# Attention with a quantised feed-forward on one core: the order of ScalarE's small copies among its exponentials

## The chip, the cores and the metric

The kernel runs on one core of one Trainium2 chip. Its engines are TensorE (matrix products, PE in the rows; PEld is its weight load), VectorE (DVE), ScalarE (ACT), GpSimd (POOL) and SyncE (SP), which issues most transfers. Each runs its own instructions in order, and they wait for each other on semaphores. The metric is the device time of the program in microseconds, the median of several executions; less is better.

## What is computed

For x of shape (8, 512, 1024) and a mask of shape (8, 1024), attention runs over the 1024 positions with 16 heads of 32 channels, and its result goes through an int8 feed-forward layer and is added to x. Cut to what matters:

```python
Q, K, V = (proj(Wq), proj(Wk), proj(Wv))              # each (8, 16, 1024, 32)
att = einsum('bhqd,bhkd->bhqk', Q, K) / sqrt(32) + b
att = softmax(att * m + (1.0 - m) * -1e30, axis=-1)   # m: the mask over keys
y = einsum('bhqk,bhkd->bhqd', att, V)                 # back to (8, 512, 1024)
scale = maximum(max(abs(y), axis=-1), 1e-7) / 127     # of each channel's row
q = clip(round(y / scale), -128, 127)
out = x + float16((q @ weight.T) * scale * w_scale + bias)
```

## The kernel before

The first part (`project`, some 590 us) makes queries, keys and values for the eight batches and stores queries and keys in DRAM, each as a high and a low part. The second part (`attend`) is what the change touches. It runs 32 steps of 53.8 us; a step is four heads of one batch. A step has 64 units, `t` from 0 to 63. A unit is one head, one tile of 128 keys and 512 of the 1024 queries: units 0 to 31 take the first query half, 32 to 63 the second, and four units in a row share a key tile.

For each unit TensorE makes a score tile of 128 by 512 (L798), which carries the mask's bias and the row's maximum in extra rows, so that ScalarE only has to take its exponential into `probs` (L932). Score tiles lie in three PSUM banks in turn: the score of unit t needs the bank that the exponential of unit t - 3 has emptied. (From unit 27 on the banks are counted one further, so unit 28 follows unit 27's.) With each unit TensorE also makes one row-maximum product (L147) into a ring of four PSUM banks, which VectorE reduces (L154). These maxima run ahead: from unit 20 (`OWN`) on they are those of the next step, heads 0 to 3 of the first query half at units 20, 28, 36 and 44, and then the second half.

The units come in bursts of eight. Behind every fourth unit of eight (3, 11, 19, 27, 35, ...) TensorE makes the weighted sums of the values for two key tiles (`weigh`, L829, 16 matmuls, 1.9 us) into the one bank `pv`. Extras stand at fixed units: the maxima are transposed at units 20 and 52 (L169), ScalarE (L176) and VectorE (L182) split them; sums of the probabilities go out at 27 and 59 (L839); the feed-forward of the step before stands at unit 59 (L872).

ScalarE walks the same units. Among its exponentials stand, at numbered units:

- `take_y` (L937), which empties `pv` into `y_raw` once a query half's weighted sums are done: at unit 3 for the step before, at unit 35 for this step's first half. It waits for TensorE's last `weigh` of that half. TensorE's next `weigh` into `pv`, at unit 43, waits for it.
- `double_k` (L963), which copies the 32 rows of the high key part of one head to other partitions, once a head, for the next step: two of them at unit 19 (heads 0 and 1), two at unit 27 (heads 2 and 3). TensorE waits for head h's copy (`k_doubled`) at the first maximum of that head, units 20, 28, 36, 44. They wait for `k_loaded`.
- `double_q2` (L973), the same for two heads of the second query half: at unit 35, behind `take_y`, and at unit 59. It waits for `q2_loaded`. TensorE's maxima of the second query half wait for it (`q2_doubled`), from unit 52 on.
- `round_rows` (L944) at unit 43 and `make_ints` (L949) at 51, which quantise.

SyncE issues the two loads of the second query half of the next step (L117) behind the store of this step's maxima (L189), which is ready a little after unit 20. GpSimd sums the probabilities (L1177), starts adding transfers among them (L1161), normalises and adds bias and residual; it waits for TensorE's weighted sums behind unit 59 once a step. The copies for a step are made in the step before; steps 1 to 30 have them at these units.

Of the kernel before, what the change touches and what calls it, by code (L numbers as in the profile page):

```python
# [28 lines left out]
GH = P // DH  # L29
# [53 lines left out]
def wait(eng, sem, value):  # L83

    if not isinstance(value, int) or value > 0:
        eng.wait_ge(sem, value)


def score_bank(s, t):

    if isinstance(s, int) and s == LAST and t > SKEW:
        return (t - SKEW - 1 + SCORES) % (SCORES + 1)
    return (t - (t > SKEW)) % SCORES
# [39 lines left out]
def landed(all_parts, n):  # L133

    return all_parts + (all_parts - 16) * (n - 1)
# [36 lines left out]
def high_max(nc, act, buf, max_parts, marks, s, chunk, maxT_done, max_rows, max_hi_done):  # L172

    act.wait_ge(maxT_done, 2 * s + chunk + 1)
    wait(act, max_rows[chunk], MAX_ROWS * s)
    nc.scalar.activation(max_parts[:, chunk, :], buf[0:2 * CHUNK, 0:P], ACT.Identity, scale=marks[:, 1:2]).then_inc(max_hi_done, 1)  # L176
# [412 lines left out]
def attend(nc, x, qk_d, v_d, bias_d, fw, ws_rep, fb_rep, out,  # L589
# [5 lines left out]
    with ExitStack() as ctx:  # L595
# [62 lines left out]
        def halves_before(s, half):  # L658

            return QH * s + half  # L660

        def pairs_before(s, half, i):

            return s * sum(i in paired for paired in PAIRED) + half * (i in PAIRED[0])

        def ring_of(use):

            return ring[PLACE[use] % RINGS]
# [14 lines left out]
        def uses(s, par):  # L683

            return (s - par) // 2 + 1
# [233 lines left out]
        @block.scalar  # L919
        def _(act):  # L920
            def exps(s, t):
                half, kt, h = t // (TT * GH), t // GH % TT, t % GH
                if h == 0:

                    wait(act, pv_done, QH * TT * s + t // GH - RING + 1)
                    before = halves_before(s, half) - 1
                    if kt in FREED[1 - half]:
                        wait(act, acc_done, ADDS * before + FREED[1 - half][kt])
                    else:
                        wait(act, pair_done[kt // 2], 16 * pairs_before(s, half, kt // 2))  # L930
                act.wait_ge(score_done, UNITS * s + t + 1)
                nc.scalar.activation(probs[:, kt, h, :], score[score_bank(s, t)][:, :], ACT.Exp).then_inc(exp_done, 1)  # L932

            def take_y(s, half):
                act.wait_ge(pv_done, QH * TT * s + (half + 1) * TT)
                wait(act, y_done, 2 * (s - 1) + half + 1)
                nc.scalar.activation(y_raw[:, half, :], pv[:, :], ACT.Copy).then_inc(y_raw_done, 1)  # L937

            def round_rows(s, cols=slice(0, T)):

                if s == 0:
                    act.wait_ge(const_set, 3)
                act.wait_ge(inv_done, s + 1)
                nc.scalar.activation(y[:, cols], y[:, cols], ACT.Identity, bias=magic[:, 0:1], scale=inv_scale[:, 0:1]).then_inc(rounded, 1)  # L944

            def make_ints(s, cols=slice(0, T)):
                act.wait_ge(rounded, s + 1)
                wait(act, qT_done, s)
                nc.scalar.activation(q_int[:, cols], y[:, cols], ACT.Identity, bias=magic[:, 1:2]).then_inc(q_done, 1)  # L949

            def store_out(s, half):
                act.wait_ge(res_done, 2 * s + half + 1)
                act.dma_start(out[s * P:(s + 1) * P, half * N:(half + 1) * N],
                              res[:, half * N:(half + 1) * N]).then_inc(out_stored, 16)

            def load_res(s):

                wait(act, out_stored, 32 * s)
                act.dma_start(res[:, :], x[s * P:(s + 1) * P, :]).then_inc(res_loaded, 16)

            def double_k(s, h):
                act.wait_ge(k_loaded[s % 2], landed(LOADS_K, uses(s, s % 2)))
                nc.scalar.activation(k_stack[s % 2][2 * DH:3 * DH, h, :], k_stack[s % 2][0:DH, h, :].bitcast(F32),  # L963
                                     ACT.Copy).then_inc(k_doubled, 1)

            def double_q1(s):
                act.wait_ge(q1_loaded[s % 2], landed(LOADS_Q, uses(s, s % 2)))
                nc.scalar.activation(q_stack[s % 2][DH:2 * DH, 0, :, :], q_stack[s % 2][0:DH, 0, :, :].bitcast(F32),
                                     ACT.Copy).then_inc(q1_doubled, 1)

            def double_q2(s, i):
                act.wait_ge(q2_loaded[s % 2], landed(LOADS_Q, uses(s, s % 2)))
                nc.scalar.activation(q_stack[s % 2][DH:2 * DH, 1, 2 * i:2 * i + 2, :],  # L973
                                     q_stack[s % 2][0:DH, 1, 2 * i:2 * i + 2, :].bitcast(F32), ACT.Copy).then_inc(q2_doubled, 1)

            def step(s, prev=True, ahead=True):
                for t in range(UNITS):
                    exps(s, t)
                    if prev and ahead and t == 19:
                        double_k(s + 1, 0)  # L980
                        double_k(s + 1, 1)
                    if prev and ahead and t == 27:
                        double_k(s + 1, 2)
                        double_k(s + 1, 3)
                    if t == GH - 1 and prev:
                        take_y(s - 1, 1)
                    if t == TURN_1:
                        high_max(nc, act, ring_of(("turn", t)), max_parts, marks, s, 1, maxT_done, max_rows, max_hi_done)
                    if t == UNITS // 2 + GH - 1:
                        take_y(s, 0)  # L990
                    if prev and ahead and t == 35:
                        double_q2(s + 1, 0)
                    if prev and ahead and t == SUMS_0:
                        double_q2(s + 1, 1)
                    if s + 2 < STEPS and t == SUMS_0:
                        double_q1(s + 2)
                    if t == ROUND and prev:
                        round_rows(s - 1)
                    if t == INTS and prev:
                        make_ints(s - 1)  # L1000
                        if s >= 2:
                            store_out(s - 2, 1)
                    if t == SUMS_0 and prev:
                        load_res(s - 1)
                    if t == TURN_0 and ahead:
                        high_max(nc, act, ring_of(("turn", t)), max_parts, marks, s + 1, 0, maxT_done, max_rows, max_hi_done)

            for i in range(2):
                act.wait_ge(part_stored[i], 16 * B * STAGES)
            for s in range(STEPS):  # L1010
                step(s, prev=s > 0, ahead=s < LAST)
            round_rows(LAST, slice(0, N))
            make_ints(LAST, slice(0, N))
# [289 lines left out]
```

## Time and profile before

| | us |
|---|---|
| median of 3 runs | 2297.32 (2295.03 to 2297.74) |
| the profiled execution | 2295.35 |
| its span | 2293.5 |

Busy in the span: TensorE 98%, GpSimd 74%, VectorE 70%, ScalarE 67%. TensorE's share comes from matmuls whose ends are modelled, and the shares are means over two parts with different limits, so a step of the second part is read by itself: the order of each engine's instructions in time, with its idle time and who ended it. The step from 1354.00 to 1407.83 us is read below; the period is 53.81 to 53.92 us in all the steps from 1 to 30. It begins with the feed-forward at unit 59; unit 4 is at 1362.95, unit 12 at 1368.74, unit 20 at 1374.54, unit 28 at 1381.63, unit 36 at 1387.44 and unit 44 at 1394.41.

### The profile page before, as it was taken

What the parts mean: (1) busy time and instruction counts of PE and PEld (TensorE: products, weight loads), DVE (VectorE), ACT (ScalarE), POOL (GpSimd) and SP (SyncE); (2) the same over time, 40 slices, a digit from 0 to 9 for tenths busy, and PEclk for the clock granted to TensorE, in tenths of its full rate; (3) what the DMA queues carried; (4) which work ended last, traced back from release to release, by engine and by line L of the source; (5) the groups of instructions that cost most, each with busy time, mean ns of one, the idle gap of its engine ahead of it and who ended that gap; (6) DMA issues with size and microseconds to landing.
All of it is one profiled execution on the core that took longest, in us unless ns stands there. A gap on an engine that the chain in (4) does not pass through costs nothing.

```text
span 2293.5 us, 34614 instructions
## 1 busy us (share of the span) xinstructions
PE 2249.3 (98%) x11892; PEld 1354.8 (59%) x11924; DVE 1616.1 (70%) x2779; ACT 1538.4 (67%) x2681; POOL 1708.3 (74%) x735
## 2 busy tenths in 40 slices
PE   9999999999999999999999999999999999999998
PEld 7888888887555555555555555555555555555553
DVE  3311111117888888888888888888888888888883
ACT  3322222223788888887887888888888887888774
POOL 2322333322899998989999998998989989998996
PEclk9999999999999999999999999999999999999999
DMA  6665545575888888888888888888888888888874
GB/s 238 253 229 193 183 183 215 189 219 145 188 186 188 185 185 189 185 191 189 194 187 189 178 189 183 190 187 187 187 184 187 189 188 191 189 189 189 181 155 109
DMA packets 137909, 433.27 MB, mean 189 GB/s; under 512 B 12248, under 2 KB 48088, under 8 KB 113440
## 3 DMA queue, kind: packets, MB, share of 16 engines
q0 software_dynamic: 27360, 199.24, 44.2%
q1 hardware_dynamic: 101040, 205.85, 29.5%
q10 hardware_dynamic: 9360, 26.22, 3.2%
q8 instruction: 91, 1.49, 0.3%
q14 instruction: 58, 0.48, 0.1%
HBM read 130.06 MB, written 100.93 MB: 101 GB/s over the span
## 4 chain that ended last, share of the span: by engine, by line
PE 91%; ACT 3%; POOL 2%; DMA 2%; issue 1%; DVE 0%; POOLq 0%; ACTq 0%
PE score L798 21%; PE pv L829 20%; PE ring L147 19%; PE ring L344 11%; PE score L344 9%; PE ring L872 4%; PE pv L344 3%; PE ring L839 2%; POOL acc L1177 2%; DMA probs<-probs 1%; ACT q_stack L973 1%; ACT probs L932 1%; PE ring L862 1%; ACT y_raw L937 1%; PE ring L169 0%
## 5 line engine op out<-in xcount | busy, mean ns | idle before, releaser
L154 DVE TENSOR_REDUCE half_max<-ring 128x1 f32<-128x512 f32 x2048 | 1261.9, 678 | 92.2 <-PE ring L147 84.4
L932 ACT ACTIVATE probs<-score 128x512 f32<-128x512 f32 x2039 | 1032.6, 615 | 235.0 <-PE score L798 233.5
L1177 POOL TENSOR_TENSOR acc<-acc,probs 128x2048 f32<-128x2048 f32 x189 | 903.6, 4781 | 29.0 <-DMA probs<-probs 26.9
L798 PE MATMUL score<-q_stack,k_stack 100*128 100x512 f32 x2039 | 855.6, 421 | 25.0 <-ACT probs L932 25.0
L147 PE MATMUL ring<-k_stack,q_stack 98*128 98x512 f32 x2048 | 815.1, 398 | 1.7 <-issue 1.7
L798 PEld LDWEIGHTS score<-q_stack,k_stack 100*128 100x128 f32 x2039 | 383.2, 188 | 386.3 <-issue 184.4
L829 PE MATMUL pv<-probs,v_in 128*32 128x512 f32 x4096 | 492.5, 598 | 0.0
L147 PEld LDWEIGHTS ring<-k_stack,q_stack 98*128 98x128 f32 x2048 | 388.4, 190 | 65.0 <-DVE qT L1084 9.0
L1177 POOL TENSOR_TENSOR acc<-probs 128x2048 f32<-128x2048 f32 x63 | 297.8, 4727 | 30.3 <-DMA probs<-probs 15.6
L562 POOL TENSOR_TENSOR q_stack<-x_raw,k_stack 128x1024 fp32r<-128x1024 f32 x28 | 67.8, 2462 | 294.0 <-ACT k_stack L426 294.0
L1161 POOL DMA_DIRECT2D probs<-probs x190 | 192.4, 1012 | 102.8 <-PE pv L829 92.2
L829 PEld LDWEIGHTS pv<-probs,v_in 128*32 128x32 f32 x4096 | 106.9, 109 | 231.8 <-ACT probs L932 143.9
L502 DVE TENSOR_TENSOR part_lo<-score,part_hi 128x512 fp32r<-128x512 f32 x24 | 16.2, 690 | 181.1 <-ACT part_hi L453 181.1
L576 POOL TENSOR_TENSOR part_lo<-k_scaled,part_hi 128x512 fp32r<-128x512 f32 x64 | 82.3, 1304 | 55.3 <-ACT part_hi L456 55.3
L963 ACT ACTIVATE k_stack<-k_stack 32x1024 fp32r<-32x1024 f32 x120 | 120.1, 1047 | 1.5
L456 ACT ACTIVATE part_hi<-k_scaled 128x512 fp32r<-128x512 f32 x64 | 39.3, 629 | 115.9 <-DVE k_scaled L513 87.4
L872 PE MATMUL ring<-fw,qT 128*128 128x512 bf16 x480 | 108.8, 379 | 5.9 <-issue 4.9
L344 PE MATMUL ring<-q_stack,w_hi 128*128 128x512 f32 x256 | 101.3, 396 | 0.0
L344 PE MATMUL ring<-k_stack,w_lo 128*128 128x512 f32 x256 | 101.2, 395 | 0.0
L1184 POOL TENSOR_TENSOR y<-y_raw,factor 128x512 f32<-128x512 f32 x63 | 98.4, 1562 | 2.2 <-DVE factor L1037 2.2
L344 PE MATMUL ring<-k_stack,w_hi 128*128 128x512 f32 x256 | 99.5, 396 | 0.0
L1190 POOL TENSOR_TENSOR half<-prod,fb_rep 128x512 f16<-128x512 f32 x63 | 89.2, 1416 | 12.9 <-DVE prod L1089 12.9
(118 smaller groups left out, 2117.6 us busy)
## 6 DMA issues: line engine op xcount, KB each, us to landing
probs<-probs POOLq DMA_DIRECT2D x190, 1024.0 KB, 8.4
q_stack<-qk_part SPq DMA_DIRECT2D x132, 256.0 KB, 4.3
k_stack<-qk_part SPq DMA_DIRECT2D x66, 512.0 KB
qk_part<-part_hi SPq DMA_DIRECT2D x64, 512.0 KB, 2.7
qk_part<-part_lo SPq DMA_DIRECT2D x64, 512.0 KB, 3.6
v_steps<-v_out SPq DMA_DIRECT2D x64, 256.0 KB, 2.3
v_in<-v_steps SPq DMA_DIRECT2D x32, 512.0 KB, 4.7
v_out<-x ACTq DMA_DIRECT2D x31, 512.0 KB, 8.1
```

The costliest lines, as they stand in the source:

```text
L147: pe.matmul(bank[:, :], q_stack[par][0:ROW_MAX, chunk, h, qt * P:(qt + 1) * P], k_stack[par][0:ROW_MAX, h, half * N:(half + 1) * N], start ...
L154: nc.vector.tensor_reduce(half_max[:, pair // CHUNK, pair % CHUNK, half:half + 1], bank[:, :], AX_X, ALU.max, negate=True).then_inc(neg_ma ...
L344: return pe.matmul(bank[:, :], lhsT, rhs, start=(k == 0), stop=(k == 3 * CT - 1))
L798: pe.matmul(score[score_bank(s, t)][:, :], k_stack[par][0:ROWS, h, kt * P:(kt + 1) * P], q_stack[par][0:ROWS, half, h, :], start=True, sto ...
L829: mm = pe.matmul(pv[h * DH:(h + 1) * DH, :], v_in[:, par, kt % TT, h * DH:(h + 1) * DH], probs[:, kt % RING, h, :], start=(kt % TT == 0), ...
L872: mm = pe.matmul(buf[:, :], qT[:, tt, :], fw[:, tt, cols], start=(tt == 0), stop=(tt == TT - 1))
L932: nc.scalar.activation(probs[:, kt, h, :], score[score_bank(s, t)][:, :], ACT.Exp).then_inc(exp_done, 1)
L963: nc.scalar.activation(k_stack[s % 2][2 * DH:3 * DH, h, :], k_stack[s % 2][0:DH, h, :].bitcast(F32), ACT.Copy).then_inc(k_doubled, 1)
L1161: pool.dma_start(probs[:, b, :, :], probs[:, a, :, :], accum_op=ALU.add).then_inc(pair_done[i], 16)
L1177: nc.gpsimd.tensor_tensor(acc[:, half, :, :], first, probs[:, tile, :, :], ALU.add).then_inc(acc_done, 1)
L1184: nc.gpsimd.tensor_tensor(y[:, half * N:(half + 1) * N], y_raw[:, half, :], factor[:, half, :], ALU.mult).then_inc(y_done, 1)
L1190: nc.gpsimd.tensor_tensor(half16[:, half, :], prod[:, half, :], fb_rep[:, half * N:(half + 1) * N], ALU.add).then_inc(half_done, 1)
```

## The change

In ScalarE's step, three edits. `double_k` of head 1 moves from unit 19 to unit 27, where it stands ahead of those of heads 2 and 3. The `double_q2` of unit 35 is written ahead of `take_y` instead of behind it. All other work, its waits and its data stay as they are.

```diff
                     if prev and ahead and t == 19:
                         double_k(s + 1, 0)
-                        double_k(s + 1, 1)
                     if prev and ahead and t == 27:
-                        double_k(s + 1, 2)
-                        double_k(s + 1, 3)
+                        for h in range(1, GH):
+                            double_k(s + 1, h)
+                    if prev and ahead and t == 35:
+                        double_q2(s + 1, 0)
                     if t == GH - 1 and prev:
                         take_y(s - 1, 1)
...
                     if t == UNITS // 2 + GH - 1:
                         take_y(s, 0)
-                    if prev and ahead and t == 35:
-                        double_q2(s + 1, 0)
                     if prev and ahead and t == SUMS_0:
                         double_q2(s + 1, 1)
```

ScalarE's instructions around units 19 to 27, before. The first row is the exponentials of units 4 to 19, L963 the key copies, L176 the split of the maxima behind unit 20, and the seven exponentials are units 21 to 27:

```order
L932 ACTIVATE probs<-score 128x512 x16
L963 ACTIVATE k_stack<-k_stack 32x1024 x2
L932 ACTIVATE probs<-score 128x512
L176 ACTIVATE max_parts<-ring,marks 32x128
L932 ACTIVATE probs<-score 128x512 x7
L963 ACTIVATE k_stack<-k_stack 32x1024 x2
```

The same place after the change:

```order
L932 ACTIVATE probs<-score 128x512 x16
L963 ACTIVATE k_stack<-k_stack 32x1024
L932 ACTIVATE probs<-score 128x512
L176 ACTIVATE max_parts<-ring,marks 32x128
L932 ACTIVATE probs<-score 128x512 x7
L963 ACTIVATE k_stack<-k_stack 32x1024 x3
```

One key copy has gone from ahead of unit 20's exponential to ahead of unit 28's.

ScalarE's instructions around unit 35, before. The first row is the exponentials of units 28 to 35, L937 is `take_y`, L973 the query copy, and the next eight exponentials are units 36 to 43:

```order
L932 ACTIVATE probs<-score 128x512 x8
L937 ACTIVATE y_raw<-pv 128x512
L973 ACTIVATE q_stack<-q_stack 32x1024
L932 ACTIVATE probs<-score 128x512 x8
L944 ACTIVATE y<-y,magic,inv_scale 128x1024
```

After the change:

```order
L932 ACTIVATE probs<-score 128x512 x8
L973 ACTIVATE q_stack<-q_stack 32x1024
L937 ACTIVATE y_raw<-pv 128x512
L932 ACTIVATE probs<-score 128x512 x8
L944 ACTIVATE y<-y,magic,inv_scale 128x1024
```

The query copy and `take_y` have changed places. The order on TensorE, VectorE and GpSimd is the same in both kernels.

## Rows read from the trace of the kernel before

**Rows 1.** The page: busy time of each engine, and TensorE's granted clock in 40 slices.
```profile
PE 2249.3 (98%) x11892; PEld 1354.8 (59%) x11924; DVE 1616.1 (70%) x2779; ACT 1538.4 (67%) x2681; POOL 1708.3 (74%) x735
...
PEclk9999999999999999999999999999999999999999
```

**Rows 2.** Waits of TensorE over the span: us in total, times, longest us.
```profile
PE score L798 <- ACT probs L932: 25.0, 32, 0.8
```

**Rows 3.** Busy time by stretches: length, busy us (instructions) by engine, clock, DMA, GB/s.
```profile
1354.00:1407.83 53.83, 52.86 (x298) 28.48 (x298) 46.84 (x83) 43.82 (x78) 48.92 (x21) 1.00 0.87 187
```

**Rows 4.** TensorE in order of time, units 36 to 44: start, us, instruction [idle before].
```profile
1387.44 0.50 PE L798 MATMUL score<-q_stack,k_stack 100*128 100x512 f32 x1
...
1388.73 0.39 PE L147 MATMUL ring<-k_stack,q_stack 98*128 98x512 f32 x1
1389.93 0.50 PE L798 MATMUL score<-q_stack,k_stack 100*128 100x512 f32 x1 [0.81 <-ACT probs L932]
1390.27 0.40 PE L147 MATMUL ring<-k_stack,q_stack 98*128 98x512 f32 x1
...
1394.41 0.50 PE L798 MATMUL score<-q_stack,k_stack 100*128 100x512 f32 x1
```

**Rows 5.** ScalarE in order of time, behind unit 19 to unit 43, repeats merged.
```profile
1373.41 2.00 ACT L963 ACTIVATE k_stack<-k_stack 32x1024 fp32r<-32x1024 f32 x2
1375.43 0.60 ACT L932 ACTIVATE probs<-score 128x512 f32<-128x512 f32 x1
...
1376.18 3.44 ACT L932 ACTIVATE probs<-score 128x512 f32<-128x512 f32 x7
1379.64 2.00 ACT L963 ACTIVATE k_stack<-k_stack 32x1024 fp32r<-32x1024 f32 x2
1382.25 4.03 ACT L932 ACTIVATE probs<-score 128x512 f32<-128x512 f32 x8 [0.61 <-PE score L798]
1387.58 0.60 ACT L937 ACTIVATE y_raw<-pv 128x512 f32<-128x512 f32 x1 [1.30 <-PE pv L829]
1388.20 1.06 ACT L973 ACTIVATE q_stack<-q_stack 32x1024 fp32r<-32x1024 f32 x1
1389.28 4.03 ACT L932 ACTIVATE probs<-score 128x512 f32<-128x512 f32 x8
```

**Rows 6.** TensorE in order of time: units 12, 20, 23, 24, 28 and 31.
```profile
1368.74 0.50 PE L798 MATMUL score<-q_stack,k_stack 100*128 100x512 f32 x1
...
1374.54 0.50 PE L798 MATMUL score<-q_stack,k_stack 100*128 100x512 f32 x1
...
1376.43 0.40 PE L147 MATMUL ring<-k_stack,q_stack 98*128 98x512 f32 x1
1376.81 0.50 PE L798 MATMUL score<-q_stack,k_stack 100*128 100x512 f32 x1
...
1381.63 0.50 PE L798 MATMUL score<-q_stack,k_stack 100*128 100x512 f32 x1
...
1383.14 0.40 PE L798 MATMUL score<-q_stack,k_stack 100*128 100x512 f32 x1
```

**Rows 7.** ScalarE in order of time, behind unit 3 and at unit 4.
```profile
1363.08 0.60 ACT L937 ACTIVATE y_raw<-pv 128x512 f32<-128x512 f32 x1 [1.30 <-PE pv L829]
1363.58 0.59 ACT L932 ACTIVATE probs<-score 128x512 f32<-128x512 f32 x1
```

**Rows 8.** Query loads of L117: their slowest step at this place, then the line's whole span.
```profile
L117 SPq DMA_DIRECT2D q_stack<-qk_part x2: 329/352/375, 1539.1 to 1539.6; - x2
...
DMA to landing us min/median/max: 3.9/4.7/5.5
...
DMA to landing us min/median/max: 3.0/4.3/12.1
```

**Rows 9.** VectorE in order of time: the reductions of units 44 to 51.
```profile
1395.18 4.88 DVE L154 TENSOR_REDUCE half_max<-ring 128x1 f32<-128x512 f32 x8 [0.36 <-PE ring L147]
```

**Rows 10.** GpSimd in order of time: its shortest wait behind unit 59, in steps 1 to 30.
```profile
1622.79 0.85 POOL L1161 DMA_DIRECT2D probs<-probs  x1 [1.47 <-PE pv L829]
```

## The prediction

> **What bounds the kernel now.** I read the page first. TensorE is busy for 98% of the span at a granted clock of full speed, the 2.4 GHz level, in all forty slices [rows 1]; the clock is not what this change can move. Of one step of the attention part (units 0 to 63) the table by stretches shows 53.83 us, of which TensorE is busy for 52.86, GpSimd for 48.92, VectorE for 46.84, ScalarE for 43.82, and the DMA engines for 0.87 of the time [rows 3]. So TensorE sets the period, and what can be won is the time in which it stands still. Next I read who it waits for: over the whole span 25.0 us in 32 times, for ScalarE's exponentials, 0.8 us at the longest [rows 2]. The order of TensorE's work in one step then tells where: between the row maximum of unit 38 (1388.73) and the score of unit 39 (1389.93) it stands still for 0.81 us [rows 4]. The trace has this row, of 0.81 to 0.83 us, in each of the 30 steps 1 to 30; they make 24.5 of the 25.0 us.
>
> The reason is a chain of three PSUM banks. The score of unit 39 goes into the bank that the exponential of unit 36 empties. ScalarE is idle for 1.30 us behind the exponential of unit 35, until TensorE has finished the weighted sums that `take_y` copies (1387.58); then it copies, then it does the query copy of 1.06 us (1388.20), and only then the exponential of unit 36 (1389.28) [rows 5]. The query copy, which depends on none of this, stands on the path, and the hole of 1.30 us in front of it is empty.
>
> **What a stall costs beside its idle time.** Behind an undisturbed burst of eight units the next burst's first score comes 5.80 us after this one's (1368.74 to 1374.54) [rows 6]. For the burst of unit 36 it is 6.97 us (1387.44 to 1394.41) [rows 4]. The burst therefore costs 1.17 us too much and not 0.81: the first maximum behind the stall comes 0.34 us after its score (1389.93, 1390.27) [rows 4] where six matmuls take 1.51 us without a stall (1381.63 to 1383.14, its first one 0.34 as well, so 0.235 each behind it) [rows 6], the matmul in front of the stall ends earlier than its slot, and the four scores behind it follow ScalarE's pace of 0.48 us.
>
> **Part 1, the query copy in front of `take_y`.** After the change it follows the exponential of unit 35: the eight exponentials from 1382.25 last 4.03, so they end at 1386.28 [rows 5]. It is a move; nothing is added. It then holds ScalarE from 1386.3 for 1.08 (from 1388.20 to 1389.28 in rows 5) to 1387.4, and `take_y` cannot begin before 1387.58 anyway. Its cover is the 1.30 us hole, with 0.2 us left. The exponential of unit 36 comes 0.50 us behind the start of `take_y`, as at unit 4, where no copy stands between (1363.08, 1363.58) [rows 7]: at 1388.08. The release takes 0.65 us from the start of an exponential to the matmul that needs its bank (1389.28 to 1389.93) [rows 4, 5], and some 0.1 more until the stream is back in its slots, so unit 39 could go at 1388.83; undisturbed it is due 1.51 us behind 1387.44, at 1388.95 [rows 4, 6]. The stall is gone, with 0.12 us to spare: gain 1.17 us a step. The lower bound of this gain is the idle row alone, 0.81.
>
> The copy waits for the loads of the next step's second query half (`q2_loaded`). That wait now has `take_y` and the exponentials queued behind it, and TensorE behind those. In the slowest step that I found, the second of the two loads was issued at 1539.6 and landed 5.5 us later [rows 8]; three steps of 53.84 earlier this is 1383.6, and the copy is due at 1386.3, so 2.7 us are left. No cost.
>
> **Part 2, one key copy from unit 19 to unit 27.** Now two copies stand behind unit 19 (1373.41) and the exponential of unit 20 starts at 1375.43; its score was started at 1374.54 and would let it start 0.62 later (unit 28 does: 1381.63, 1382.25) at 1375.16 [rows 5, 6]. It is 0.27 late, the turned maxima follow, and unit 21's exponential is at 1376.18. TensorE pays at unit 24: 0.38 us between 1376.43 and 1376.81 in place of 0.235, and the 0.10 of a restart: 0.25 us [rows 5, 6]. With one copy this goes, as everything from unit 20 on moves 0.27 earlier on ScalarE: gain 0.25.
>
> Behind unit 27 three copies stand in place of two. The two start at 1379.64 and take 2.00, and the one before unit 20's exponential shows 2.02 from the first copy to it [rows 5]; three take about 2.99. They start 0.27 earlier, at 1379.37, so unit 28's exponential starts at 1382.36, while its score, 0.25 earlier, has it ready at 1382.00. It is 0.36 late. Unit 31's score needs its bank at 1383.14 less 0.25, 1382.89, and can go at 1382.36 plus 0.74, 1383.10 [rows 5, 6]: 0.21 lost, and four more units at ScalarE's 0.48 in place of 0.47 and a late weight load at the end lose some 0.07. The second part thus gives 0.25 and takes 0.28: net minus 0.03. The bounds are plus 0.25 (nothing lost at unit 31) and minus 0.25 (the gain at unit 24 absent). The key copies' own reader is no cost: TensorE takes head 1 behind unit 28's score (1381.63) and that copy now ends near 1380.4; heads 2 and 3 are taken at units 36 and 44.
>
> **The sum.** 1.17 less 0.03 is 1.14 us in each of 30 steps, 34.2 us. The profiled execution took 2295.35, so 2261.1; the median lies 2.0 above it, and the forecast is 2263.1.
>
> **What is late next.** GpSimd keeps its place from step to step by one wait, for TensorE's weighted sums behind unit 59; its idle time there was 1.47 us in the tightest of the steps [rows 10], and about 3.5 in most. 1.14 fits in. VectorE is closer: behind unit 43 it waits 0.36 us for TensorE [rows 9], and that wait will be about zero, since it has all of its work of unit 39 (maximum of the outputs, scales) still to do while TensorE comes 1.17 earlier. Then only the four ring banks, nearly two units of room, stand between a late reduction and TensorE.
>
> A rule of the Trainium skill speaks here ("Perfetto Trace Analysis", section "Identifying the Most-Contended Engine"): TensorE's busy share is no good measure, since pipelined matmuls are misread, while for GpSimd occupancy is a fair one; the most occupied engine is to be improved first. By that rule GpSimd (48.92 of 53.83) would be the bound and a better order on ScalarE would bring little. This trace speaks against it, since GpSimd waits for TensorE in every step; it is rival 3 below.
>
> **Rivals.**
> 1. VectorE or a rest of the stall takes part of the gain in the second half of the step, so that only about the idle row comes back: 0.81 times 30 is 24.3, time 2273. For it: VectorE's vanished slack [rows 9]. Against: four banks. Chance 0.16.
> 2. Unit 31 loses nothing: 1.17 plus 0.25 is 1.42, times 30 is 42.6, time 2254.7. For it: unit 20's exponential, 0.27 late in the trace, goes by without idle time of TensorE in front of unit 23, which waits for it; the bubble comes at unit 24. Against: 0.36 is more than 0.27. Chance 0.12.
> 3. GpSimd becomes the bound, because its transfers land later when they are asked for in less time: the gain shrinks to under 0.5 us a step, 2282 to 2297. Chance 0.05, since it needs its 1.47 to 4 us of slack gone.
> 4. Slower: a late load holds the query copy, and with it `take_y`. The longest landing on that line is 12.1 us [rows 8]; issued at 1378.1 (1539.6 less three steps) it is there at 1390.2, `take_y` starts at 1391.3 and unit 36's exponential at 1391.8 in place of 1389.28: 2.5 us a step, 75 us, time 2372 if it is so in all steps. It decides from a landing of 9.6 us after the issue on. The 12.1 is of other loads on the same line; those at this place took up to 5.5. Chance 0.03.
> 5. The move has no effect, because the 1.30 us hole isn't idle on ScalarE but hides a release that the copy only shifts: time 2297. Against: unit 3 shows the same hole and no stall. Chance 0.02.
>
> **How the numbers follow.** Forecast, 2259 to 2268: 0.62. From 0.2% on (4.6 us, about what a measurement of this kernel tells from no change) it counts as faster: forecast and rivals 1 and 2, and most of 3, 0.94; within 0.2%: 0.03; slower 0.03. Leaving out rivals 3 to 5 leaves 0.9, so the range runs from 2254 (rival 2) to 2273 (rival 1).
>
> **What would show it.** Right: TensorE's waits for the exponentials fall from 25.0 us to below 5; the query copy starts right behind unit 35's exponential, `take_y` at its old place behind unit 35's weighted sums; period 52.7; a small bubble at unit 31 and none at unit 24. Wrong: idle time in front of the query copy (rival 4), TensorE's weight loads waiting for VectorE's reductions (rival 1), GpSimd's wait behind unit 59 at zero (rival 3).

## The result

| | us |
|---|---|
| before, median of 7 runs | 2296.71 (2295.03 to 2301.94) |
| changed, median of 7 runs | 2303.70 (2295.93 to 2304.62) |
| ratio changed to before | 1.002, 95% interval 1.001 to 1.0029 |
| the changed kernel's profiled execution | 2295.93 (its span 2294.1) |

The change made the kernel slower by 0.2% (0.3% between the two medians), where I had forecast 1.5% faster. The profiled execution is the fastest of the seven, 8 us under the median; the other six lie between 2302.9 and 2304.6. So the trace below shows the mechanism, but less of the loss than the median holds: its execution is only 0.6 us longer than the one profiled before.

The page of the changed kernel has VectorE, ScalarE and GpSimd about as busy as before, and TensorE 12.7 us busier [rows 1]:

```profile
span 2294.1 us, 34646 instructions
PE 2262.0 (99%) x11924; PEld 1359.3 (59%) x11924; DVE 1612.4 (70%) x2779; ACT 1541.7 (67%) x2681; POOL 1709.8 (75%) x735
```

TensorE has no more work than before. Its 32 more instructions are records of the feed-forward that are missing in the trace before (7.3 us), and the row maxima (L147) show 13.7 us more for the same 2048 matmuls, which is where the new waits are.

The waits over the span (us in total, times, longest) show that the stall which the change aimed at is gone, 25.0 us in [rows 2] and 0.4 now, and what has come in its place:

```profile
POOL acc L1176 <- DMA probs<-probs: 110.3, 73, 10.5
...
DVE absmax L1041 <- POOL y L1183: 45.4, 36, 10.2
...
ACT y L944 <- DVE inv_scale L1054: 27.7, 15, 7.5
...
PE ring L147 <- DVE half_max L154: 14.8, 19, 1.8
...
PE ring L798 <- ACT probs L932: 4.0, 2, 3.8
...
PE score L798 <- ACT probs L932: 0.4, 2, 0.2
```

Before, the first three were these:

```profile
POOL acc L1177 <- DMA probs<-probs: 42.5, 60, 2.8
...
DVE absmax L1042 <- POOL y L1184: 8.9, 2, 7.5
ACT y L944 <- DVE inv_scale L1055: 8.4, 2, 7.6
```

GpSimd waits 68 us more for its adding transfers, VectorE 37 us more for GpSimd's normalised outputs (L1183, `normalise`), ScalarE 19 us more for the scales that VectorE makes of them (L1054), and TensorE waits for VectorE's reductions.

**The steps fall into two kinds.** From one feed-forward's start to the next, the 29 steps before took 53.81 to 53.92 us. Now eleven of the first 29 take 52.62 to 52.74 us, as forecast, while thirteen take 53.5 to 56.8, with stalls of TensorE around unit 24 or 44 or both; the mean is 53.77, against 53.85 before. First a step that went as it should have, ScalarE in order of time from behind unit 27 on, the rows that answer to [rows 5]:

```profile
1055.31 2.95 ACT L963 ACTIVATE k_stack<-k_stack 32x1024 fp32r<-32x1024 f32 x3
1058.28 4.03 ACT L932 ACTIVATE probs<-score 128x512 f32<-128x512 f32 x8
1062.33 1.05 ACT L973 ACTIVATE q_stack<-q_stack 32x1024 fp32r<-32x1024 f32 x1
1063.54 0.60 ACT L937 ACTIVATE y_raw<-pv 128x512 f32<-128x512 f32 x1 [0.16 <-PE pv L829]
1064.04 4.02 ACT L932 ACTIVATE probs<-score 128x512 f32<-128x512 f32 x8
```

The query copy fills the hole in front of `take_y`, 0.16 us of it is left (forecast 0.2), and unit 36's exponential follows `take_y` by 0.50. TensorE's scores of units 20, 28, 31, 36 and 44 in the same step answer to [rows 4, 6]:

```profile
1050.48 0.50 PE L798 MATMUL score<-q_stack,k_stack 100*128 100x512 f32 x1
...
1057.30 0.50 PE L798 MATMUL score<-q_stack,k_stack 100*128 100x512 f32 x1
...
1058.93 0.50 PE L798 MATMUL score<-q_stack,k_stack 100*128 100x512 f32 x1
...
1063.41 0.50 PE L798 MATMUL score<-q_stack,k_stack 100*128 100x512 f32 x1
...
1069.20 0.50 PE L798 MATMUL score<-q_stack,k_stack 100*128 100x512 f32 x1
```

Units 36 to 44 take 5.79 us instead of 6.97: 1.18 won, forecast 1.17. Units 20 to 28 take 6.82 instead of 7.09: 0.27 won, forecast 0.25. Units 28 to 36 take 6.11 instead of 5.81: 0.30 lost, forecast 0.28, though not where I had put it: unit 31's score comes 0.12 late (1.63 behind unit 28's in place of 1.51; forecast 0.21), and the other 0.18 is lost behind it. Each of the three parts came out to within 0.02 us, and the means over all eleven such steps are the same to 0.01.

**The loop that binds now.** GpSimd in order of time in the same step, from one issue of pair 1's transfer for the second half to the next. (Pair i is the adding transfer of key tile 2i onto 2i + 1, L1160 here. Pair 1 of the second half is the last but one issued in a step, ahead of GpSimd's wait behind unit 59; GpSimd's second sum of the half needs it.)

```profile
1025.98 1.26 POOL L1160 DMA_DIRECT2D probs<-probs  x1
1029.59 0.86 POOL L1160 DMA_DIRECT2D probs<-probs  x1 [2.34 <-PE pv L829]
...
1036.18 4.58 POOL L1176 TENSOR_TENSOR acc<-acc,probs 128x2048 f32<-128x2048 f32 x1 [1.17 <-DMA probs<-probs]
...
1054.96 4.58 POOL L1176 TENSOR_TENSOR acc<-probs 128x2048 f32<-128x2048 f32 x1 [0.40 <-DMA probs<-probs]
...
1076.05 4.59 POOL L1176 TENSOR_TENSOR acc<-acc,probs 128x2048 f32<-128x2048 f32 x1 [1.17 <-DMA probs<-probs]
1080.59 0.86 POOL L1160 DMA_DIRECT2D probs<-probs  x1
```

GpSimd waits 2.34 us for TensorE behind unit 59 (1029.59), which reads as slack. But it is no slack: the transfer of pair 1 has been issued in front of that wait (1025.98), and its landing, 10 us later, holds the second sum (1036.18) whatever TensorE does. Had TensorE come 1 us earlier and the landing stayed where it was, the 2.34 would be 1.34 and the 1.17 would be 2.17. From there on everything on GpSimd follows in one chain: sum, bias and residual, sum, pair 0 and its landing (0.40), sums, normalising, pair 3 and its landing (1.17), the last sum, and pair 1 again. One turn took 54.61 us (1025.98 to 1080.59), while TensorE's step took 52.63. Such a turn puts GpSimd 2 us behind TensorE. The next turn takes 51.69 us; over the 29 steps the turns lie between 50.5 and 58.0, and their mean is that of the steps, 53.8.

A slow step shows how this reaches TensorE. VectorE takes the maximum of each output half at fixed places in its order, at units 19 and 39, and there waits for GpSimd's `normalise`. The step from 973.1 on, GpSimd first, then VectorE, then TensorE:

```profile
980.72 4.59 POOL L1176 TENSOR_TENSOR acc<-acc,probs 128x2048 f32<-128x2048 f32 x1 [2.42 <-DMA probs<-probs]
...
1001.90 4.60 POOL L1176 TENSOR_TENSOR acc<-probs 128x2048 f32<-128x2048 f32 x1 [2.87 <-DMA probs<-probs]
...
1011.60 1.57 POOL L1183 TENSOR_TENSOR y<-y_raw,factor 128x512 f32<-128x512 f32 x1
```

```profile
994.50 0.69 DVE L1041 TENSOR_REDUCE absmax<-y 128x1 f32<-128x512 f32 x1 [0.59 <-POOL y L1183]
...
1013.21 0.69 DVE L1041 TENSOR_REDUCE absmax<-y 128x1 f32<-128x512 f32 x1 [2.88 <-POOL y L1183]
```

```profile
1015.07 0.47 PE L147 MATMUL ring<-k_stack,q_stack 98*128 98x512 f32 x1 [1.70 <-DVE half_max L154]
```

Two landings cost GpSimd 2.42 and 2.87 us, its output comes at 1013.2, VectorE stands still for 2.88 us with the ring's maxima behind it, the four ring banks fill, and TensorE stands still for 1.70 us at unit 44.

There is a second way, and it shows in the step behind the 29, the 30th. The scales wait for the same maximum, ScalarE's rounding (L944, unit 43) waits for the scales, and the exponentials stand behind the rounding. ScalarE, then TensorE:

```profile
2252.33 1.24 ACT L944 ACTIVATE y<-y,magic,inv_scale 128x1024 f32<-128x1024 f32 x1 [3.58 <-DVE inv_scale L1054]
```

```profile
2254.10 0.80 PE L798 MATMUL ring<-q_stack,k_stack 100*128 100x512 f32 x1 [3.79 <-ACT probs L932]
```

Before, the two waits at this place were 0.88 and 1.07 us. This step took 56.1 us, before 51.9. So in the profiled execution the 29 steps together are 2.3 us shorter than before, and the 30th alone is 4.2 us longer.

**The clock falls behind such a stall.** TensorE's table by stretches (length, busy us by engine, granted clock, DMA, GB/s) around it:

```profile
1012.90:1016.30 3.40, 1.70 (x10) 0.88 (x7) 3.03 (x7) 1.93 (x3) 3.40 (x5) 1.00 0.19 39
1016.40:1019.80 3.40, 3.40 (x9) 2.56 (x9) 3.40 (x7) 2.46 (x5) 3.40 (x2) 0.50 1.14 231
```

In the first stretch TensorE is busy for 1.70 of 3.40 us; in the second it runs at the 1.2 GHz level and makes 9 matmuls. At the 2.4 GHz level it makes 14 in that time (0.235 us each), so such a fall costs up to 1.7 us more, on top of the stall (an estimate: half of the 3.4). The granted clock shows 0.50 in the same way at 1716 and 1986 us, behind stalls of 1.56 and 1.75 us, and for 6.8 us from 2252.0 on, inside the stall of 3.79; behind a stall of 1.26 us it did not fall. In the attention part of the kernel before it fell in the last 1.3 us alone. The length of a stall does not settle it: in the traces of the experiments below, stalls of 1.78 us (`after_add_cut`, at 1015.6) and 2.25 us (`after_absmax_late`, at 1722.4) had no fall behind them, and one of 1.19 us (`after_pair2_later`, at 1448.3) had. The mean granted clock of the seven runs is 0.993 to 0.998.

### The profile page after: what moved, and what is told of

It reads as the page before. It is cut to its first block, busy times and chain, and to the rows that moved or that the text cites. A ratio compares the mean times of both kernels' runs of the same rounds, so it can differ in the third digit from the quotient of the medians.

```text
span 2294.1 us, 34646 instructions
## 1 busy us (share of the span) xinstructions
PE 2262.0 (99%) x11924; PEld 1359.3 (59%) x11924; DVE 1612.4 (70%) x2779; ACT 1541.7 (67%) x2681; POOL 1709.8 (75%) x735
## 4 chain that ended last, share of the span: by engine, by line
PE 83%; issue 7%; POOL 4%; DMA 3%; ACT 2%; DVE 1%; POOLq 0%; ACTq 0%
PE score L798 18%; PE ring L147 17%; PE pv L829 16%; PE ring L344 11%; PE score L344 9%; PE ring L872 4%; DMA probs<-probs 3%; PE pv L344 3%; PE ring L839 2%; POOL acc L1176 2%; ACT probs L932 1%; POOL y L1183 1%; PE ring L862 1%; DVE absmax L1041 1%; DVE half_max L154 0%
## 5 line engine op out<-in xcount | busy, mean ns | idle before, releaser
L147 PE MATMUL ring<-k_stack,q_stack 98*128 98x512 f32 x2048 | 828.8, 405 | 16.6 <-DVE half_max L154 14.8
L147 PEld LDWEIGHTS ring<-k_stack,q_stack 98*128 98x128 f32 x2048 | 390.3, 191 | 112.1 <-DVE half_max L154 45.1
L1160 POOL DMA_DIRECT2D probs<-probs x190 | 194.8, 1026 | 44.7 <-PE pv L829 37.3
L963 ACT ACTIVATE k_stack<-k_stack 32x1024 fp32r<-32x1024 f32 x120 | 120.2, 1047 | 1.5
L872 PE MATMUL ring<-fw,qT 128*128 128x512 bf16 x512 | 116.1, 380 | 0.8 <-DVE qT L1083 0.8
L1183 POOL TENSOR_TENSOR y<-y_raw,factor 128x512 f32<-128x512 f32 x63 | 98.5, 1563 | 2.1 <-DVE factor L1036 2.1
```

What stands on the lines that cost most here:

```text
L147: pe.matmul(bank[:, :], q_stack[par][0:ROW_MAX, chunk, h, qt * P:(qt + 1) * P], k_stack[par][0:ROW_MAX, h, half * N:(half + 1) * N], start ...
L872: mm = pe.matmul(buf[:, :], qT[:, tt, :], fw[:, tt, cols], start=(tt == 0), stop=(tt == TT - 1))
L1160: pool.dma_start(probs[:, b, :, :], probs[:, a, :, :], accum_op=ALU.add).then_inc(pair_done[i], 16)
L1183: nc.gpsimd.tensor_tensor(y[:, half * N:(half + 1) * N], y_raw[:, half, :], factor[:, half, :], ALU.mult).then_inc(y_done, 1)
```

## The experiments

Theory A, formed from the rows above: GpSimd and its adding transfers form a loop that takes 53 to 55 us a step, the 53.85 of TensorE before hid it, and it binds once TensorE wants 52.7. The rivals: the key copies' move costs (B), the clock falls for another reason and is the cause (C), GpSimd's total work is the bound (D), and some more that stand with their runs. Controls apply the same edit to the kernel before.

### The two parts apart

`q_only` takes the query copy alone (the edit is against the changed kernel):

```diff
                     if prev and ahead and t == 19:
                         double_k(s + 1, 0)
+                        double_k(s + 1, 1)
                     if prev and ahead and t == 27:
-                        for h in range(1, GH):
-                            double_k(s + 1, h)
+                        double_k(s + 1, 2)
+                        double_k(s + 1, 3)
```

> Only the query copy in front of take_y at unit 35; the key copies as before. Theory A (a GpSimd and transfer loop of 53.5 to 54 us a step has become the bound: pair 1's transfer of the second half, issued in front of GpSimd's wait behind unit 59, lands too late for the second sum): the stall at unit 39 goes, steps of 52.7 us alternate with late ones, and the time is within 0.4% of before, 2290 to 2305. Rival B (moving three key copies behind unit 27 is what costs; the query copy alone brings 1.1 us a step): 2262 to 2266.

Measured: 2299.60 us, ratio 1.0014 (1.0004 to 1.0023). Rival B falls: the query copy alone, forecast to gain 35 us, loses 3 to 4. `k_only` takes the other part alone, from the kernel before:

```diff
                     if prev and ahead and t == 19:
                         double_k(s + 1, 0)
-                        double_k(s + 1, 1)
                     if prev and ahead and t == 27:
-                        double_k(s + 1, 2)
-                        double_k(s + 1, 3)
+                        for h in range(1, GH):
+                            double_k(s + 1, h)
```

> Only head 1's key copy from unit 19 to unit 27; the query copy stays behind take_y. Theory A: TensorE's period stays at 53.8 us or so, GpSimd keeps its slack, 2294 to 2299. Rival B (the key copies cost): 2335, since it would have to eat the 34 us of the query copy and 7 more.

Measured: 2295.88 us, ratio 0.9999 (0.9989 to 1.0008), clock 0.999, the stall at unit 39 in every step as before. Where unit 39's stall sets the step, the key copies are worth nothing either way.

### Taking work out of the loop, and beside it

`after_bias_cut` shortens GpSimd's bias addition, which lies in the loop. It leaves out the bias on 448 of each 512 columns in all steps but the last (one memset at the start fills them):

```diff
...
-                nc.gpsimd.tensor_tensor(half16[:, half, :], prod[:, half, :], fb_rep[:, half * N:(half + 1) * N],
+                few = 64 if s is not LAST else N
+                nc.gpsimd.tensor_tensor(half16[:, half, 0:few], prod[:, half, 0:few], fb_rep[:, half * N:half * N + few],
                                         ALU.add).then_inc(half_done, 1)
```

> The changed kernel, with GpSimd's bias addition cut to 64 of 512 columns in all steps but the last (work left out: the bias on 448 columns of each half). It takes about 1.2 us twice a step out of GpSimd's chain between the landing of pair 1 and its next issue. Theory A: the loop falls under TensorE's 52.7 us: 2262 to 2268, no long stalls at units 24 and 40, clock 0.999. Rival C (TensorE's clock, which falls in some stretches of the changed kernel for another reason, costs the time): as the changed kernel, 2300 or more.

Measured: 2260.78 us, ratio 0.9849 (0.9833 to 0.9866). All 29 steps of its trace take 52.63 to 52.81 us, and the clock's mean is 0.999. In the trace a shortened addition takes 0.96 us less on the mean, twice a step. The whole forecast gain is there as soon as these 1.9 us of GpSimd's chain are gone, so nothing on TensorE, ScalarE or VectorE hindered it. Rival C falls: with the same order on TensorE and ScalarE the granted clock stays at 1.00 through all the steps read (it falls only in the last 4 us of the span), and the gain is there. Not every fall needs the change: `k_only` and `before_bias_cut`, with the old order of the query copy, have one of 3.4 us in the last step too (at 2242 and 2237).

`before_bias_cut`, the control, is the same edit in the kernel before.

> Control: the kernel before, with the same bias addition cut to 64 of 512 columns in all steps but the last. Theory A: before, TensorE's own 53.85 us a step bind and GpSimd has room, so nothing is won: 2293 to 2297. Rival E (GpSimd's chain was the bound already before, and the cut brings the same at any order of ScalarE's copies): 2262.

Measured: 2294.75 us, ratio 0.9994 (0.9984 to 1.0003). Before, GpSimd did not bind.

`after_add_cut` takes about as much work out, but where GpSimd waits for pair 1's landing anyway. It leaves out two of the four heads in the first addition of each second half, 2.2 us:

```diff
...
-                nc.gpsimd.tensor_tensor(acc[:, half, :, :], first, probs[:, tile, :, :], ALU.add).then_inc(acc_done, 1)
+                heads = slice(0, 2) if (half, k) == (1, 0) else slice(0, GH)
+                first = probs[:, FIRST, heads, :] if k == 0 else acc[:, half, heads, :]
+                nc.gpsimd.tensor_tensor(acc[:, half, heads, :], first, probs[:, tile, heads, :], ALU.add).then_inc(acc_done, 1)
```

> The changed kernel, with the first addition of each second half cut to two of its four heads (work left out: tile 6 and tile 1 of heads 2 and 3 in the row sums of second halves). It takes about 2.4 us out of GpSimd's work, but at the place where GpSimd waits for pair 1's landing anyway. Theory A: the wait grows by what the addition loses, and the time stays near the changed kernel's, 2295 to 2304. Rival D (GpSimd's busy time as a whole is the bound, wherever it is spent): as the bias cut, 2262 to 2268.

Measured: 2295.19 us, ratio 0.9997 (0.9985 to 1.001). GpSimd in order of time, the second sum in the step that answers to the slow one above:

```profile
981.15 4.58 POOL L1179 TENSOR_TENSOR acc<-acc,probs 128x2048 f32<-128x2048 f32 x1 [4.83 <-DMA probs<-probs]
```

The wait has grown from 2.42 to 4.83 us, by at least what the addition lost. Over the span GpSimd's waits for its transfers grew from 110.3 to 162.7 us, by most of the 67 us by which its additions are shorter. Rival D falls: 2.2 us a step less work brought 8.5 us of the median here against the changed kernel, and 1.9 us less brought 43 us at the other place. The Trainium skill ("Perfetto Trace Analysis", section "Identifying the Most-Contended Engine") would have the engine with the highest occupancy improved first, and calls occupancy a fair measure for GpSimd. It would have pointed to the right engine, which I had dismissed. But these two runs show that occupancy does not say what to take off it: GpSimd is busy for 49.0 of 52.6 us in a good step and was for 48.9 of 53.8 before, when it did not bind [rows 3], and what binds is its work and the transfers' landings in one chain.

### Moving things in the loop, with all work kept

`after_fill` puts work into the wait for pair 1's landing:

```diff
-                if prev:
-                    add(s - 1, 1, 1)
                 if second:
                     add_bias(s - 2, 0)
                     add_residual(s - 2, 0)
                 if prev:
+                    add(s - 1, 1, 1)
                     add(s - 1, 1, 2)
```

> The changed kernel, complete, with GpSimd's bias and residual additions of the first half (2.6 us) in front of the second sum of the second half, where it stood idle for pair 1's landing, instead of behind it. Theory A: pair 1 may land 2.6 us later without holding GpSimd, the loop is shorter by 2.6 us than TensorE's period needs, and TensorE's 52.7 us a step bind: 2260 to 2266, clock 0.999, no waits over 0.5 us at units 24 and 40. Rival D (GpSimd's total work is what binds): no change against the changed kernel, 2300 to 2305, since it does exactly the same work.

Measured: 2264.66 us, ratio 0.9868 (0.9851 to 0.9884), with the whole computation. GpSimd in its trace, one step:

```profile
1017.59 1.31 POOL L1160 DMA_DIRECT2D probs<-probs  x1
1021.58 0.86 POOL L1160 DMA_DIRECT2D probs<-probs  x1 [2.69 <-PE pv L829]
1022.14 4.87 POOL L1176 TENSOR_TENSOR acc<-probs 128x2048 f32<-128x2048 f32 x1
1026.65 1.61 POOL L1189 TENSOR_TENSOR half<-prod,fb_rep 128x512 f16<-128x512 f32 x1
1028.42 1.16 POOL L1197 TENSOR_TENSOR v_out<-v_out,half 128x512 f32<-128x512 f32 x1 [0.16 <-POOL half L1189]
1029.54 4.61 POOL L1176 TENSOR_TENSOR acc<-acc,probs 128x2048 f32<-128x2048 f32 x1
```

Pair 1's transfer again takes 10.0 us (its landing in the trace), but the second sum starts 11.95 us behind the issue without a wait, as bias and residual lie between. The 29 steps take 52.67 to 52.80. `q_only_fill` has the same fill, and only the query copy moved.

> The same fill, with only the query copy moved and the key copies as before. It measures what the key copies' move is worth where TensorE binds. From my sum (0.25 won at unit 24, 0.28 lost at unit 31) within 2 us of the run with both, 2260 to 2267; if unit 31 loses nothing, 7 us slower than it.

Measured: 2263.64 us, ratio 0.9862 (0.9845 to 0.9878). Most of its steps take 52.67 to 52.70 against 52.70 to 52.73 with the key copies moved: the key copies' move costs 0.03 us a step, as the sum had it, which is less than the whole times can tell apart. Three of its steps take 53.1 to 55.0, with a stall of 1.21 us for VectorE's reductions in one of them: the fill leaves the loop some room, but not much. `before_fill` is the control.

> Control: the same fill in the kernel before. TensorE binds there with 53.85 us a step and GpSimd's wait behind unit 59 has room: 2293 to 2297.

Measured: 2296.00 us, ratio 0.9999 (0.999 to 1.0009). Neither edit brings anything alone; together they bring 1.3 to 1.4%.

`after_pair_early` issues pair 1 earlier instead:

```diff
                 begin_pair(s, 1, 0)
-                add(s, 0, 3)
                 if ahead:
                     begin_pair(s, 1, 1)
+                add(s, 0, 3)
+                if ahead:
                     begin_pair(s, 1, 2)
```

> The changed kernel, complete, with GpSimd issuing pair 1's transfer of the second half ahead of its last addition of the first half instead of behind it. No work is taken out. GpSimd then waits some 2 us for TensorE's weighted sums behind unit 51, of the 3 it had left behind unit 59, and the transfer starts 4 us earlier and no longer beside pair 2's. Theory A: the late landing is out of the loop, and the time is 2262 to 2272. Rival F (GpSimd's work alone, not the landing, is what the loop consists of): 2295 to 2305, since its work is the same and it waits once more.

Measured: 2282.43 us, ratio 0.9934 (0.9912 to 0.9955): faster than both kernels, but 10 us above the expectation and 18 us short of `after_fill`. GpSimd's waits for its transfers have fallen from 110.3 to 30.3 us over the span, and a new wait has come, TensorE's for the stored maxima of the next step (SyncE's small transfer at L189), at unit 0, 9.8 us in 15 times:

```profile
1460.03 0.50 PE L798 MATMUL score<-q_stack,k_stack 100*128 100x512 f32 x1 [0.55 <-DMA q_stack<-max_parts]
```

That transfer was issued at 1448.41, and pairs 0 and 1 were now both under way (issued at 1444.43 and 1447.24). `before_pair_early` is the control.

> Control: the kernel before with the same earlier transfer of pair 1. Theory A: TensorE's own stall at unit 39 still sets the period of 53.85: 2293 to 2297. Rival H (the earlier transfer shortens any order): 2285 or less.

Measured: 2301.92 us, ratio 1.0027 (1.0017 to 1.0038), slower than both expectations: I had not counted the small transfer. Five of its first 29 steps are 0.6 to 1.3 us longer than 53.85, with a gap at the same place beside that of unit 39.

`after_pair2_later` asks what makes pair 1's landing long, by issuing pair 2 behind the first sum instead of in front of it:

```diff
                 if prev:
+                    begin_pair(s - 1, 1, 2)
                     add(s - 1, 1, 1)
...
                     begin_pair(s, 1, 1)
-                    begin_pair(s, 1, 2)
                     add(s, 1, 0)
```

> The changed kernel, complete, with pair 2's transfer of the second half issued behind GpSimd's first addition of that half (5 us later) instead of in front of it, so that pair 1's, issued 1.6 us before it, travels without it at first. It asks whether pair 1's long landing (9.9 us on the mean, against 8.3 for pair 0's) is due to its company. If it is: pair 1 lands in some 8.3 us, the loop is 1.5 us shorter, time 2265 to 2280. If it isn't: landing stays at 9.5 or more and the time at 2295 to 2304. Pair 2's own landing is needed 9 us after its issue, which may turn into a wait at the third sum.

Measured: 2299.78 us, ratio 1.0014 (1.0002 to 1.0026). Pair 1's mean landing is 9.4 us instead of 9.7, with pair 2 issued 7 us behind it. So it is as long when pair 2 isn't beside it for most of its way, and pair 2 is refuted as what makes it long; what does stays open.

### Taking away the way to TensorE

`after_absmax_late` lets VectorE take the first output half's maximum later, at unit 31 instead of 19:

```diff
-                    if t == TURN_1 - 1 and prev:
-                        take_absmax(s - 1, 0)
-                        take_floor(s - 1)
...
                     if t == SUMS_1 + 4 and prev:
                         spread(s - 1, 1)
+                        take_absmax(s - 1, 0)
+                        take_floor(s - 1)
```

> The changed kernel, with VectorE's maximum of the first output half moved from unit 19 to unit 31. It takes away the way in which a late GpSimd reaches TensorE at unit 24 (VectorE waits for the normalised outputs, the ring of maxima fills). Theory A: GpSimd's loop is as long as before, so TensorE is held elsewhere (unit 40, sums behind 27 and 59); a small gain, 2285 to 2300. Rival G (the wait at unit 20 alone is the cost): 2262 to 2268.

Measured: 2308.00 us, ratio 1.0042 (1.0022 to 1.0063), worse than expected. The stalls at unit 24 are gone from its trace, and those around unit 44 are longer and more: in eight of 29 steps two matmuls there stand 1.7 to 2.8 us apart, in the changed kernel in four. Rival G falls, and it fits a loop: what TensorE doesn't wait for at one place it waits for at the next. That it costs 4 us more than the changed kernel I had not foreseen; the longer stalls bring falls of the clock with them (mean 0.994), but how much is theirs these runs don't part.

## Why the prediction was wrong

- **What bounds the kernel before, the cost of the stall (1.17 us and not 0.81), the query copy's cover, the 0.50 and 0.65 us links, the loads' margin:** right. The good steps show 1.18 us, and no step shows the query copy waiting for its loads (rival 4). The hole in front of `take_y` was idle and took the copy (rival 5).
- **The key copies, net minus 0.03 us a step:** right, 0.27 won and 0.30 lost in the trace, 0.03 between `after_fill` and `q_only_fill`. That the 0.21 at unit 31 was 0.12 and the 0.07 behind it 0.18 cancels out; so far the match is luck. Rival 2 fell.
- **The sum, 34.2 us:** right as TensorE's share. With GpSimd's loop relieved the kernel takes 2260.8 to 2264.7 us, forecast 2263.1.
- **"What is late next" is the step that failed.** It read GpSimd's wait behind unit 59, 1.47 us at the least and some 3.5 in most steps [rows 10], as room for 1.14. The wait stands beside a transfer in flight that doesn't depend on it. The room was what lies between pair 1's landing and the second sum. Before, over the 29 steps, the landing came 4.6 us after the feed-forward's start on the mean, and the second sum at 5.1 where nothing held it: 0.5 us. The trace before says so in GpSimd's rows. At the start of the step that I had read, pair 1 is issued at 1348.99, lands 9.2 us later, at 1358.2, and is needed at 1359.11. In another step (the last two rows) it lands 10.3 us after its issue and holds the second sum for 1.69 us; in eleven of the 29 steps it held it for 0.3 us or more. I had used the issue alone. By this estimate, taking 1.14 us a step from a loop with 0.5 us of room could have given at most 0.5. The rows:

```profile
1348.99 0.85 POOL L1161 DMA_DIRECT2D probs<-probs  x1
1353.59 0.86 POOL L1161 DMA_DIRECT2D probs<-probs  x1 [3.75 <-PE pv L829]
...
1359.11 4.60 POOL L1177 TENSOR_TENSOR acc<-acc,probs 128x2048 f32<-128x2048 f32 x1
...
1727.16 1.13 POOL L1161 DMA_DIRECT2D probs<-probs  x1
...
1737.60 4.60 POOL L1177 TENSOR_TENSOR acc<-acc,probs 128x2048 f32<-128x2048 f32 x1 [1.69 <-DMA probs<-probs]
```

- **Rival 3, given 0.05, is what happened, and its end was too low.** I had it end at no change (2297). A loop that runs late does not merely give the gain back. The mean time to landing of pair 1 went from 9.3 to 9.7 us and that of pair 2 from 11.5 to 13.5, TensorE's waits come in lumps of up to 1.8 us in the 29 steps and of 3.8 in the 30th, and behind some of them the clock falls. The reason given against it, that GpSimd waits for TensorE in every step, is the same misreading.
- **Rival 1 (VectorE takes part of the gain):** wrong as priced. With GpSimd relieved (`after_bias_cut`, `after_fill`) TensorE has no stall for VectorE's reductions in the attention part. It is VectorE, though, through which GpSimd's lateness reaches TensorE. The margin of its first maximum I had not worked out: in the step read before, `normalise` ended at 1372.94 and the maximum began at 1374.57, 1.6 us later.

**Open:** what makes the other executions 8 us longer than the profiled one. In the profiled one three falls of 3.4 us at half clock (1016, 1716, 1986) cost up to 5 us, and the one of 6.8 at 2252 up to 3.4 more. But the falls are not what makes the others slower: the slowest of the seven (2304.62 us) had a mean granted clock of 0.998, and the profiled one, the fastest, 0.995. A clock of 0.998 leaves at most some 5 us to the falls (an estimate: 0.002 of the time), so without them that execution would still have taken 2300 us, and the gain of 34 us would be gone all the same. The slower runs have no rows of their own. Open is also what stretches a transfer's landing from 7 us to 10 or more.

## What to carry to other kernels

An engine's wait is slack only if nothing that it needs later was started ahead of that wait: for each asynchronous transfer, take the time from its landing to its first use, not the idle time of the engine that issued it, and add up one turn of the chain through the landings before trusting that the next engine has room. Where a fix on the first bound gains nothing, keep it and look for the second: here moving two instructions on GpSimd into the time of a landing, worth nothing alone, made the same fix worth 1.4%. And an engine that is made late may cost more than it gave, if its waits come in lumps that others turn into stalls.

## What the runs showed of the hardware

Three things I had not expected: Stalls of TensorE of 1.56, 1.70 and 1.75 us were each followed by some 3.4 us at the 1.2 GHz level, in a kernel in which it is busy for 99% of the time; one of 1.26 us was not, nor was one of 2.25 us in another run. The adding transfers of 1 MB took from 6.9 us to 13.8 from issue to landing before the change, and their place in the step goes with it (7.2 us on the mean for one, 11.5 for another). And a transfer of 16 KB issued among two of them held TensorE until 11.6 us after its issue.
